# Token stages of a two-layer metaformer kernel: the second product one step later and first in the order, centring and variance as 48-channel blocks in four 64x64 tiles

## The chip, the cores and the metric

The program runs on one core of one Trainium2 chip. The metric is the device time of one execution, in microseconds. Engines are named as in the profile: PE is TensorE, PEld its weight loads, DVE is VectorE, ACT is ScalarE, POOL is GpSimd, SP is SyncE, which issues most of the DMAs here. Half a per cent of the time, some 13 us, is about what a measurement of this kernel can tell from no change.

## What is computed

The input is `x`, 4 images of 48 channels and 128 x 128 pixels. Two layers follow, each a convolution block and a feed-forward block on the pixels as tokens. Cut to what matters:

```
def _qlinear(x, W, b):
    y = q_acc(jnp.einsum('bsk,nk->bsn', q_mul(x), q_mul(W)))
    return q_acc(y + q_mul(b))
h = jax.nn.relu(_qlinear(x, W1, b1))
y = _qlinear(h, W2, b2)
...
x = x + _L0_conv_ref(_ln_c(x), ...)
t = _to_tokens(x)
t = t + _L0_ffn_ref(_ln_t(t), ...)
x = _from_tokens(t, x)
x = x + _L1_conv_ref(_ln_c(x), ...)
t = _to_tokens(x)
t = t + _L1_ffn_ref(_ln_t(t), ...)
```

`q_mul` rounds to an 8-bit float (5 exponent, 2 mantissa bits), `q_acc` to a 16-bit one. `_ln_t` and `_ln_c` are layer norms over the 48 channels of a pixel. The feed-forward block goes from 48 to 192 channels and back.

## The kernel before

The program is a row of stages with a barrier between them: `expand` (norm and the first product of layer 0), `gated_conv`, `token_mix` called as mix0, `wavelet` (the convolution block of layer 1), `attention_maps`, `fusion`, and `token_mix` called again as mix1. The change touches `token_mix` alone.

`token_mix` works on 64 items (2N with N = HW/NT = 32). An item is 512 pixels of two images: image h = 0 stands on partitions 0 to 47 and image h = 1 on partitions 64 to 111, so that most tiles are 112 x 512. For each item:

- `project` (L858, L861 in mix0; L864 in mix1) makes the last product of the convolution block in `x1_bank`; `add_residual` (L1012, L1014; L1017) adds the residual and writes `x1`, which has four buffers.
- `centre_in` (L869) subtracts the channel mean by a product with the 112 x 112 matrix `center`; ACT squares the result (`square`, L932); `variance("in")` (L887) is a product with `average`, written into `x1_bank` again; ACT makes logarithm (L939, `mix_logv`) and exponential (L942, `mix_rstd`); `quantize_norm` (L1025) makes the 8-bit `xq`.
- `hide(0)` and `hide(1)` (L900) are the two halves of the first product, `round_hidden` (L949) rounds each to 16 bits, `bias_hidden` (L1031) and `quantize_hidden` (L1039) make the 8-bit `hq`.
- `show` (L912) is the second product, in `x2_bank`; `round_shown` (L955) makes `y16`; `add_shown` makes `yb` (L1045) and then `x2` (L1050), which is stored.
- In mix0 alone a second norm follows for the next stage: `centre_out` (L875), `square("out")`, `variance("out")` (L887, into `x2_bank` again), logarithm, exponential and `normalise` (L1059, `mix_xn`).

The order of the work is written out by hand. `staged` takes for each engine a list of (stage, piece); in step k every piece with stage s works on item k - s, in the order of the list. A step of the steady loop so holds one call of each piece, each for another item. The engines are held together by semaphores. Those that matter here: `show` waits for `y16_ready` and, in mix0, for `logged["out"]` (the logarithm of the step before, which reads the bank that `show` writes); `variance("in")` of item k - 1 waits for `x1_ready` of item k, since it writes the bank that `add_residual` of item k reads; `add_residual` of item k waits for `x2_ready` of item k - 4, which read the same buffer of `x1`; `hide(1)` in mix0 waits for the rounding of `hide(0)`. SP loads item k in step k and stores `x2` and `xn` some steps later, in one queue.

Of the kernel before, what the change touches and what calls it, by code (L numbers as in the profile page):

```python
# [16 lines left out]
HID = 96  # L17
# [657 lines left out]
def token_mix(nc, t, tag, src, wT, bias, res, w1T, b1, w2T, b2, dst, norm_dst):  # L675
# [9 lines left out]
    with ExitStack() as st:  # L685
        k = Bench(nc, st, tag)
        center, average = k.sb("center", [CP, CP]), k.sb("average", [CP, CP])
# [10 lines left out]
        LEAD = 12 if wide else 4  # L698
# [26 lines left out]
        bank = [k.ps(f"bank{j}") for j in range(8 - 2 - 2 * len(norms))]  # L725
# [31 lines left out]
        with nc.Block() as block:  # L757
            @block.sync
            def _(sp):
                sp.wait_ge(prepared, 1)  # L760
                sp.dma_start(center[:, :], const(t, "center")[0:CP]).then_inc(weights_in, 16)
# [56 lines left out]
                def store_norm(at):  # L818
                    sp.wait_ge(xn_ready, at.n + 3)
                    for h in range(2):  # L820
                        rows = slice(PADH * h, PADH * h + C)
# [12 lines left out]
                staged(sp, 2 * N, SLOTS, [(0, load), (4, store_x2)] + [(7, store_norm)] * wide, LEAD)  # L834
# [8 lines left out]
            def _(pe):  # L843
# [22 lines left out]

                def centre_in(at):
                    pe.wait_ge(x1_ready, at.n + 1)
                    pe.matmul(centre_bank["in"][at.pair][0:CP, :], center[:, :], x1[at.slot][:, :],  # L869
                              start=True, stop=True).then_inc(centered["in"], 1)  # L870

                def centre_out(at):
                    pe.wait_ge(x2_ready, at.n + 1 + SLOTS)
                    pe.wait_ge(xn_ready, at.n + 1)
                    pe.matmul(centre_bank["out"][at.pair][0:CP, :], center[:, :], x2[at.pair][:, :],  # L875
                              start=True, stop=True).then_inc(centered["out"], 1)

                def variance(v):
                    def piece(at):
# [7 lines left out]
                        pe.matmul(var_bank[v][0:CP, :], average[:, :], sq[v][at.pair][:, :],  # L887
# [3 lines left out]
                def hide(m):  # L891


                    def piece(at):
                        pe.wait_ge(xq_ready, at.n + 1)
                        if m == 1 and len(bank) == 2:
                            pe.wait_ge(h16_ready, 4 * at.n + 2)
# [18 lines left out]
                pieces = [(0, project), (3, show), (2, hide(0)), (2, hide(1)), (1, variance("in")), (0, centre_in)]  # L916
                if norm_dst is not None:
                    pieces = [(0, project), (3, show), (2, hide(0)), (4, centre_out), (2, hide(1)), (1, variance("in")), (5, variance("out")), (0, centre_in)]
# [3 lines left out]
            def _(act):  # L922
# [41 lines left out]
            def _(dve):  # L964
                dve.memset(eps[:, 0:1], 1e-5)
                dve.memset(eps[:, 1:2], 1e-6)
                dve.memset(w1q[:, :, :, :], 0.0)
# [60 lines left out]
                def bias_hidden(at):  # L1028
                    for m in range(2):
                        dve.wait_ge(h16_ready, 4 * at.n + 2 * m + 2)  # L1030
# [31 lines left out]
                pieces = [(0, add_residual), (3, add_shown), (2, bias_hidden), (2, quantize_hidden), (1, quantize_norm)]  # L1062
                if norm_dst is not None:
                    pieces.append((5, normalise))
# [1267 lines left out]
```

## Time and profile before

| | |
|---|---|
| median of 3 runs | 2622.84 us (2618.95 to 2629.99) |
| profiled execution | 2624.89 us |
| its span, first to last instruction | 2623.1 us |
| busy shares | PE 87%, PEld 48%, DVE 58%, ACT 43%, POOL 17% |
| mix0 in the trace | from about 812 us to 1297 us |
| mix1 in the trace | from about 2232 us to the end |

The busy time is how long an engine has an instruction under way. It is a mean over stages that have different limits, so the two token stages are read by themselves: by the busy time in windows, and by the timeline of one step, which gives for each instruction its start, its duration and what its engine waited for.

### The profile page before, as it was taken

To read this page: it belongs to the slowest core of one execution; us is meant where nothing else is said; L and a number is where in the kernel's file an instruction comes from. 1 tells how busy PE (TensorE), PEld (TensorE's weight loads), DVE (VectorE), ACT (ScalarE), POOL (GpSimd) and SP (SyncE) were. 2 spreads that over 40 slices of the span, in tenths; PEclk is the share of its full clock that TensorE was granted. 3 is DMA by queue.
4 is the path that set the end of the run, shared out by engine and by line. 5 is a ranking of instruction groups with operands and counts; after the bars stand their busy time and mean duration, and the time that the engine had idled before them with its cause. 6 is when DMAs were issued, how large, how long until landed. Compare 5 with 4: busy or idle time off the path is not lost. (4 is left out here: it accounts for less than half of the span.)

```text
span 2623.1 us, 62156 instructions
## 1 busy us (share of the span) xinstructions
PE 2272.7 (87%) x21290; PEld 1247.5 (48%) x21290; DVE 1523.5 (58%) x2653; ACT 1123.3 (43%) x2338; POOL 450.0 (17%) x707
## 2 busy tenths in 40 slices
PE   6679778898996999999699999999976998688886
PEld 3344436667773333333266666666641232233332
DVE  3345401111113777777488888888842455577776
ACT  4346421111112888888532222222211111577776
POOL 7510015100100000000054444444410000000000
PEclk9789869999997999999899999999987999899999
DMA  6999989788874777877576666666628999333332
GB/s 154 260 254 270 253 284 303 230 263 262 285 245 91 142 142 146 152 142 145 100 155 144 142 142 142 142 143 143 144 86 162 240 267 237 87 102 106 105 102 78
DMA packets 533239, 458.55 MB, mean 175 GB/s; under 512 B 316476, under 2 KB 445444, under 8 KB 529778
## 3 DMA queue, kind: packets, MB, share of 16 engines
q1 hardware_dynamic: 462882, 425.87, 63.4%
q0 software_dynamic: 5744, 23.34, 3.7%
q10 hardware_dynamic: 64512, 7.88, 2.3%
q8 instruction: 78, 1.28, 0.2%
q14 instruction: 23, 0.19, 0.0%
HBM read 272.33 MB, written 186.40 MB: 175 GB/s over the span
## 5 line engine op out<-in xcount | busy, mean ns | idle before, releaser
L604 PE MATMUL gate_ps<-gate_data,gate_wt 64*64 64x289 f32 x6144 | 397.1, 416 | 39.2 <-issue 27.2
L604 PEld LDWEIGHTS gate_ps<-gate_data,gate_wt 64*64 64x64 f32 x6144 | 303.1, 136 | 134.3 <-issue 59.8
L662 DVE TENSOR_TENSOR gate_out<-gate_gelu,gate_ps 128x578 f32<-128x578 f32 x96 | 72.2, 756 | 399.3 <-PE gate_ps L604 343.7
L949 ACT CAST mix_h<-mix_bank 96x512 f16<-96x512 f32 x512 | 267.6, 593 | 7.1 <-PE mix_bank L900 3.2
L639 ACT ACTIVATE gate_gelu<-gate_ps 128x578 f32<-128x578 f32 x96 | 62.7, 653 | 367.8 <-PE gate_ps L604 331.2
L2036 PE MATMUL fus_bank<-fus_xt,fus_taps 76*32 76x512 f32 x1344 | 159.6, 626 | 28.4 <-DMA fus_shift<-gate_shift 23.5
L1031 DVE TENSOR_SCALAR mix_hb<-mix_h,mix_b1q 96x1024 f16<-96x1024 f16 x256 | 122.7, 479 | 93.6 <-ACT mix_h L949 93.6
L900 PE MATMUL mix_bank<-mix_xq,mix_w1q 112*96 112x512 fp8e5 x512 | 143.5, 382 | 29.1 <-ACT mix_h L949 23.0
L1039 DVE CAST mix_hq<-mix_hb 96x2048 fp8e5<-96x2048 f16 x128 | 156.5, 1223 | 19.5 <-DVE mix_hb L1031 16.9
L292 DVE COPY exp_out<-exp_y 128x384 f32<-128x384 f32 x192 | 102.1, 567 | 103.5 <-PE exp_y L255 52.1
L912 PE MATMUL mix_x_bank<-mix_hq,mix_w2q 96*112 96x512 fp8e5 x512 | 136.1, 388 | 29.9 <-DVE mix_hq L1039 27.7
L255 PE MATMUL exp_y<-exp_win,exp_xb 48*128 48x192 f32 x1024 | 114.2, 359 | 49.8 <-DVE exp_out L292 30.9
L869 PE MATMUL mix_centre_in<-mix_x,mix_center 112*112 112x512 f32 x256 | 134.6, 608 | 2.1 <-DVE mix_x L1014 1.2
L1517 PE MATMUL wav_full_bank<-wav_halves,wav_base_w 80*32 80x256 f32 x2304 | 136.3, 382 | 0.1
L887 PE MATMUL mix_x_bank<-mix_sq_in,mix_average 112*112 112x512 f32 x256 | 132.9, 601 | 2.1 <-DVE mix_x L1014 1.2
L955 ACT CAST mix_y<-mix_x_bank 112x512 f16<-112x512 f32 x128 | 74.9, 585 | 139.5 <-PE mix_x_bank L912 139.5
L255 PEld LDWEIGHTS exp_y<-exp_win,exp_xb 48*128 48x128 f32 x1024 | 88.9, 199 | 89.8 <-ACT exp_out L292 53.4
L864 PE MATMUL mix_x_bank<-mix_sc,mix_proj 112*112 112x512 f32 x128 | 73.7, 658 | 58.3 <-ACT mix_logv_in L939 37.1
L1458 PE MATMUL wav_front<-wav_strips,wav_front_w 48*32 48x256 f32 x3840 | 117.3, 383 | 0.0
L1663 POOL TENSOR_TENSOR wav_pool<-wav_scaled,wav_diag 128x256 f32<-128x256 f32 x96 | 68.6, 736 | 265.0 <-ACT wav_scaled L1572 264.7
L900 PEld LDWEIGHTS mix_bank<-mix_xq,mix_w1q 112*96 112x96 fp8e5 x512 | 58.1, 123 | 116.7 <-issue 82.3
L2036 PEld LDWEIGHTS fus_bank<-fus_xt,fus_taps 76*32 76x32 f32 x1344 | 44.8, 113 | 138.2 <-issue 135.1
(226 smaller groups left out, 4050.6 us busy)
## 6 DMA issues: line engine op xcount, KB each, us to landing
y<-exp_out SPq DMA_DIRECT2D x64, 816.0 KB, 12.2
gate_data<-y SPq DMA_DIRECT2D x24, 2176.0 KB, 17.6
g<-gate_out SPq DMA_DIRECT2D x48, 578.0 KB, 4.9
mix_sc<-g SPq DMA_DIRECT2D x31, 816.0 KB
gate_wt<-wm SPq DMA_DIRECT2D x96, 256.0 KB, 8.5
wav_strips<-xp SPq DMA_DIRECT2D x96, 204.0 KB, 3.8
wav_halves<-xp SPq DMA_DIRECT2D x48, 340.0 KB
init<-wav_init SPq DMA_DIRECT2D x48, 268.0 KB, 2.4
```

The costliest lines, as they stand in the source:

```text
L255: mm = pe.matmul(ps_y[h][q % 2][:, O2 * x:O2 * (x + 1)], xb[u][rows, 2 * q + x].rearrange("c s y x -> c (s y x)"), win[rows, :], start=Tru ...
L604: mm = pe.matmul(banks(a, v)[64 * g:64 * (g + 1), r], wt[q][64 * r:64 * (r + 1), 2 * a + g, n, :], src, start=n == 0, stop=n == 3)
L869: pe.matmul(centre_bank["in"][at.pair][0:CP, :], center[:, :], x1[at.slot][:, :], start=True, stop=True).then_inc(centered["in"], 1)
L887: pe.matmul(var_bank[v][0:CP, :], average[:, :], sq[v][at.pair][:, :], start=True, stop=True).then_inc(var[v], 1)
L900: pe.matmul(bank[(2 * m + h) % len(bank)][0:HID, :], w1q[:, h, m, :], xq[at.pair][:, :], start=True, stop=True).then_inc(hidden, 1)
L912: mm = pe.matmul(x2_bank[0:CP, :], w2q[:, h, m, :], hq[at.pair][:, m, h, :], start=(h + m == 0), stop=(h + m == 2))
L949: act.copy(h16[at.pair][:, m, h, :], bank[(2 * m + h) % len(bank)][0:HID, :]).then_inc(h16_ready, 1)
L1031: relu = dve.tensor_scalar(hb[at.pair][:, m, :, :].rearrange("p h n -> p (h n)"), h16[at.pair][:, m, :, :].rearrange("p h n -> p (h n)"), ...
L1039: dve.tensor_copy(hq[at.pair][:, :, :, :].rearrange("p m h n -> p (m h n)"), hb[at.pair][:, :, :, :].rearrange("p m h n -> p (m h n)"), sa ...
L1458: x = pe.matmul(half(u, r, 0, Q0)[STRIP * g:STRIP * (g + 1)], front_w[u][64 * r:64 * r + K0, 2 + dx, :], strips[u][64 * r:64 * r + K0, g, ...
L1517: x = pe.matmul(images(full_bank[u][STRIP * g:STRIP * (g + 1), :])[:, :, e::2], base_w[u][:, e, dx, :], halves[u][:, g, :, 1 + dx:1 + dx + ...
L2036: mm = pe.matmul(bank[u][0][STRIP * s:STRIP * (s + 1), :], taps[u][0:K2, dx, :], xt[u][:, s, :, dx:dx + W], start=dx == 0, stop=dx == TAPS ...
```

## The change

- The second product and all behind it move one stage later: `show`, `round_shown` and `add_shown` from stage 3 to 4, the second norm from 4 and 5 to 5 and 6, the stores from 4 and 7 to 5 and 8.
- `show` and `add_shown` go to the head of the lists of PE and DVE (`round_shown` was at the head of ACT's list already). In mix0 `project` goes behind `hide(0)`, and `variance("out")` and `centre_out` stand next to each other.
- `centre_in` and `centre_out` are two products of 64 x 64 tiles each, which also swap the halves (image 0 goes to partitions 64 to 111 of `centre_bank` and back), `variance` two products on the diagonal tiles. `pe.sem_inc(pe_turn, 1)` stands ahead of each. The weights of `hide` and the stores of `xn` are swapped to match.
- The four hidden banks become pairs of 1024 columns: one semaphore count and one ACT copy of 1024 columns per `hide` in place of two of 512.
- `quantize_hidden` waits for `mixed` of two items before. The written-out head of mix1's loop has 8 steps in place of 4.

```
-        LEAD = 12 if wide else 4
+        LEAD = 12 if wide else 8
...
-        bank = [k.ps(f"bank{j}") for j in range(8 - 2 - 2 * len(norms))]
+        pairs = [k.ps(f"bank{j}", (128, 2 * NT)) for j in range(3 - len(norms))]
...
-                staged(sp, 2 * N, SLOTS, [(0, load), (4, store_x2)] + [(7, store_norm)] * wide, LEAD)
+                staged(sp, 2 * N, SLOTS, [(0, load), (5, store_x2)] + [(8, store_norm)] * wide, LEAD)
...
+                def exchange(v, at, x):
+                    pe.sem_inc(pe_turn, 1)
+                    pe.matmul(centre_bank[v][at.pair][PADH:CP, :], center[0:C, 0:C], x[0:C, :], start=True, stop=True)
+                    pe.matmul(centre_bank[v][at.pair][0:PADH, :], center[PADH:CP, PADH:128], x[PADH:CP, :],
+                              start=True, stop=True).then_inc(centered[v], 1)
...
-                        pe.matmul(var_bank[v][0:CP, :], average[:, :], sq[v][at.pair][:, :],
+                        pe.sem_inc(pe_turn, 1)
+                        pe.matmul(var_bank[v][0:PADH, :], average[0:C, 0:PADH], sq[v][at.pair][0:C, :], start=True, stop=True)
+                        pe.matmul(var_bank[v][PADH:CP, :], average[PADH:CP, PADH:CP], sq[v][at.pair][PADH:CP, :],
                                   start=True, stop=True).then_inc(var[v], 1)
...
-                            pe.matmul(bank[(2 * m + h) % len(bank)][0:HID, :], w1q[:, h, m, :], xq[at.pair][:, :],
-                                      start=True, stop=True).then_inc(hidden, 1)
+                            mm = pe.matmul(pairs[m % len(pairs)][0:HID, NT * h:NT * (h + 1)], w1q[:, 1 - h, m, :],
+                                           xq[at.pair][:, :], start=True, stop=True)
+                        mm.then_inc(hidden, 1)
...
-                pieces = [(0, project), (3, show), (2, hide(0)), (2, hide(1)), (1, variance("in")), (0, centre_in)]
+                pieces = [(4, show), (0, project), (2, hide(0)), (2, hide(1)), (1, variance("in")), (0, centre_in)]
...
-                        for h in range(2):
-                            act.wait_ge(hidden, 4 * at.n + 2 * m + h + 1)
-                            act.copy(h16[at.pair][:, m, h, :], bank[(2 * m + h) % len(bank)][0:HID, :]
-                                     ).then_inc(h16_ready, 1)
+                        act.wait_ge(hidden, 2 * at.n + m + 1)
+                        act.copy(h16[at.pair][:, m, :, :].rearrange("p h n -> p (h n)"), pairs[m % len(pairs)][0:HID, :]
+                                 ).then_inc(h16_ready, 1)
...
+                    if not isinstance(at.n, int) or at.n >= 2:
+                        dve.wait_ge(mixed, at.n - 1)
...
-                pieces = [(0, add_residual), (3, add_shown), (2, bias_hidden), (2, quantize_hidden), (1, quantize_norm)]
+                pieces = [(4, add_shown), (0, add_residual), (2, bias_hidden), (2, quantize_hidden), (1, quantize_norm)]
```

The order of the instructions on PE, one step of mix0's loop. Before:

```order
L858 MATMUL mix_x_bank<-mix_sc,mix_proj 48x448 x2
L861 MATMUL mix_x_bank<-mix_sc,mix_proj 48x64 x2
L912 MATMUL mix_x_bank<-mix_hq,mix_w2q 112x512 x4
L900 MATMUL mix_bank<-mix_xq,mix_w1q 96x512 x2
L875 MATMUL mix_centre_out<-mix_x,mix_center 112x512
...
L900 MATMUL mix_bank<-mix_xq,mix_w1q 96x512 x2
L887 MATMUL mix_x_bank<-mix_sq_in,mix_average 112x512
L887 MATMUL mix_x_bank<-mix_sq_out,mix_average 112x512
L869 MATMUL mix_centre_in<-mix_x,mix_center 112x512
```

and with the change, from its `show` on (its line numbers are those of the changed kernel):

```order
L919 MATMUL mix_x_bank<-mix_hq,mix_w2q 112x512 x4
L906 MATMUL mix_bank<-mix_xq,mix_w1q 96x512 x2
L858 MATMUL mix_x_bank<-mix_sc,mix_proj 48x448 x2
L861 MATMUL mix_x_bank<-mix_sc,mix_proj 48x64 x2
L892 MATMUL mix_x_bank<-mix_sq_out,mix_average 64x512
L893 MATMUL mix_x_bank<-mix_sq_out,mix_average 48x512
L869 MATMUL mix_centre_out<-mix_x,mix_center 48x512
L870 MATMUL mix_centre_out<-mix_x,mix_center 64x512
L906 MATMUL mix_bank<-mix_xq,mix_w1q 96x512 x2
L892 MATMUL mix_x_bank<-mix_sq_in,mix_average 64x512
L893 MATMUL mix_x_bank<-mix_sq_in,mix_average 48x512
L869 MATMUL mix_centre_in<-mix_x,mix_center 48x512
```

`show` stood behind `project` and now opens the step; the second norm's variance came behind the first norm's and now stands with its centring ahead of the second half of `hide`.

The order on DVE, the head of a step of mix0's loop. Before:

```order
L1012 TENSOR_TENSOR mix_x<-mix_x_bank,mix_rs 112x4x7x16
L1014 TENSOR_TENSOR mix_x<-mix_x_bank,mix_rs 112x64
L1045 TENSOR_SCALAR mix_yb<-mix_y,mix_b2q 112x512
L1050 TENSOR_TENSOR mix_x<-mix_yb,mix_x 112x512
L1030 ISA
```

and with the change:

```order
L1054 TENSOR_SCALAR mix_yb<-mix_y,mix_b2q 112x512
L1059 TENSOR_TENSOR mix_x<-mix_yb,mix_x 112x512
L1004 REGISTER_ALU
L1019 TENSOR_TENSOR mix_x<-mix_x_bank,mix_rs 112x4x7x16
L1021 TENSOR_TENSOR mix_x<-mix_x_bank,mix_rs 112x64
```

The addition of the residual, which came first, now stands behind the two instructions of `add_shown`.

## Rows read from the trace of the kernel before

**Rows 1.** Windows: length, busy PE, PEld, DVE, ACT, POOL (instructions), PE clock, DMA, GB/s.

```profile
10.00:20.00 10.00, 6.03 (x7) 2.27 (x8) 0.00 (x0) 1.72 (x3) 9.70 (x13) 1.00 0.65 105
720.00:800.00 80.00, 77.90 (x1243) 61.43 (x1239) 15.09 (x20) 12.40 (x19) 0.00 (x0) 0.98 0.62 215
900.00:1260.00 360.00, 335.53 (x1237) 139.05 (x1235) 281.41 (x466) 316.44 (x569) 0.00 (x0) 1.00 0.77 147
2260.00:2600.00 340.00, 285.29 (x847) 115.04 (x847) 265.50 (x423) 253.25 (x482) 0.00 (x0) 1.00 0.37 103
```

**Rows 2.** Timeline of PE in mix0: start us, us, engine, line, operation [idle before].

```profile
1007.08 1.02 PE L887 MATMUL mix_x_bank<-mix_sq_in,mix_average 112*112 112x512 f32 x2
...
1008.80 1.02 PE L869 MATMUL mix_centre_in<-mix_x,mix_center 112*112 112x512 f32 x2
1009.75 0.98 PE L858 MATMUL mix_x_bank<-mix_sc,mix_proj 96*48 96x448 f32 x4
...
1010.77 1.07 PE L912 MATMUL mix_x_bank<-mix_hq,mix_w2q 96*112 96x512 fp8e5 x4
1011.68 0.60 PE L900 MATMUL mix_bank<-mix_xq,mix_w1q 112*96 112x512 fp8e5 x2
...
1014.01 1.02 PE L887 MATMUL mix_x_bank<-mix_sq_in,mix_average 112*112 112x512 f32 x2
```

**Rows 3.** Timeline of ACT in the same step of mix0.

```profile
1008.14 0.69 ACT L939 ACTIVATE mix_logv_in<-mix_x_bank,mix_eps 112x512 f32<-112x512 f32 x1
...
1009.40 0.67 ACT L939 ACTIVATE mix_logv_out<-mix_x_bank,mix_eps 112x512 f32<-112x512 f32 x1
...
1011.88 0.58 ACT L955 CAST mix_y<-mix_x_bank 112x512 f16<-112x512 f32 x1 [0.66 <-PE mix_x_bank L912]
```

**Rows 4.** Timeline of DVE in the same step of mix0.

```profile
1011.37 0.95 DVE L1012 TENSOR_TENSOR mix_x<-mix_x_bank,mix_rs 112x448 f32<-112x448 f32 x1
1012.23 0.27 DVE L1014 TENSOR_TENSOR mix_x<-mix_x_bank,mix_rs 112x64 f32<-112x64 f32 x1
1012.50 0.35 DVE L1045 TENSOR_SCALAR mix_yb<-mix_y,mix_b2q 112x512 f16<-112x512 f16 x1
1012.88 0.69 DVE L1050 TENSOR_TENSOR mix_x<-mix_yb,mix_x 112x512 f32<-112x512 f16 x1
```

**Rows 5.** Timeline of one step of mix1: PE and ACT.

```profile
2406.99 1.04 PE L912 MATMUL mix_x_bank<-mix_hq,mix_w2q 96*112 96x512 fp8e5 x4 [0.29 <-DVE mix_hq L1039]
...
2408.07 0.58 ACT L955 CAST mix_y<-mix_x_bank 112x512 f16<-112x512 f32 x1 [1.39 <-PE mix_x_bank L912]
2408.55 2.04 ACT L949 CAST mix_h<-mix_bank 96x512 f16<-96x512 f32 x4
2410.46 0.72 ACT L939 ACTIVATE mix_logv_in<-mix_x_bank,mix_eps 112x512 f32<-112x512 f32 x1
2411.21 0.63 ACT L942 ACTIVATE mix_rstd_in<-mix_logv_in 112x512 f32<-112x512 f32 x1
2411.74 0.58 ACT L932 ACTIVATE mix_sq_in<-mix_centre_in 112x512 f32<-112x512 f32 x1
```

**Rows 6.** Timeline of DVE in the same step of mix1.

```profile
2405.62 1.22 DVE L1039 CAST mix_hq<-mix_hb 96x2048 fp8e5<-96x2048 f16 x1 [0.15 <-DVE mix_hb L1031]
...
2407.37 0.74 DVE L1017 SCALAR_TENSOR_TENSOR mix_x<-mix_x_bank,mix_pbias,mix_rs 112x512 f32<-112x512 f32 x1
2408.69 0.35 DVE L1045 TENSOR_SCALAR mix_yb<-mix_y,mix_b2q 112x512 f16<-112x512 f16 x1 [0.59 <-ACT mix_y L955]
2409.19 0.69 DVE L1050 TENSOR_TENSOR mix_x<-mix_yb,mix_x 112x512 f32<-112x512 f16 x1
...
2411.26 1.22 DVE L1039 CAST mix_hq<-mix_hb 96x2048 fp8e5<-96x2048 f16 x1 [0.15 <-DVE mix_hb L1031]
```

**Rows 7.** Line L567 of gated_conv: duration ns min/median/max, first and last start us.

```profile
L567 PE MATMUL gate_ps<-gate_maps x20: 1056/1056/1057, 341.2 to 345.5; 2*32 2x512 f32 x20
```

**Rows 8.** Waits of SP's queue in steady mix0: us in total, times, longest.

```profile
SPq L816 <- DVE mix_x L1050: 127.6, 50, 5.1
```

More of the change, by code:

```diff
@@ L686, in token_mix @@
         k = Bench(nc, st, tag)
-        center, average = k.sb("center", [CP, CP]), k.sb("average", [CP, CP])
+        center, average = k.sb("center", [CP, 128]), k.sb("average", [CP, CP])
         eps = k.sb("eps", [128, 2])
@@ L820, in store_norm @@
                     for h in range(2):
-                        rows = slice(PADH * h, PADH * h + C)
+                        rows = slice(PADH * (1 - h), PADH * (1 - h) + C)
                         def keep(y, first, n):
@@ L865, in project @@
                     mm.then_inc(projected, 1)
+                def exchange(v, at, x):
[3 more added lines that the diff above has]
+                              start=True, stop=True).then_inc(centered[v], 1)
                 def centre_in(at):
                     pe.wait_ge(x1_ready, at.n + 1)
-                    pe.matmul(centre_bank["in"][at.pair][0:CP, :], center[:, :], x1[at.slot][:, :],
-                              start=True, stop=True).then_inc(centered["in"], 1)
+                    exchange("in", at, x1[at.slot])
                 def centre_out(at):
@@ L874, in centre_out @@
                     pe.wait_ge(xn_ready, at.n + 1)
-                    pe.matmul(centre_bank["out"][at.pair][0:CP, :], center[:, :], x2[at.pair][:, :],
-                              start=True, stop=True).then_inc(centered["out"], 1)
+                    exchange("out", at, x2[at.pair])
                 def variance(v):
@@ L895, in piece @@
                         pe.wait_ge(xq_ready, at.n + 1)
-                        if m == 1 and len(bank) == 2:
-                            pe.wait_ge(h16_ready, 4 * at.n + 2)
+                        if m == 1 and len(pairs) == 1:
+                            pe.wait_ge(h16_ready, 2 * at.n + 1)
                         pe.sem_inc(pe_turn, 1)
                         for h in range(2):
-                            pe.matmul(bank[(2 * m + h) % len(bank)][0:HID, :], w1q[:, h, m, :], xq[at.pair][:, :],
-                                      start=True, stop=True).then_inc(hidden, 1)
+                            mm = pe.matmul(pairs[m % len(pairs)][0:HID, NT * h:NT * (h + 1)], w1q[:, 1 - h, m, :],
+                                           xq[at.pair][:, :], start=True, stop=True)
+                        mm.then_inc(hidden, 1)
                     return piece
@@ L914, in show @@
                     mm.then_inc(mixed, 1)
-                pieces = [(0, project), (3, show), (2, hide(0)), (2, hide(1)), (1, variance("in")), (0, centre_in)]
+                pieces = [(4, show), (0, project), (2, hide(0)), (2, hide(1)), (1, variance("in")), (0, centre_in)]
                 if norm_dst is not None:
-                    pieces = [(0, project), (3, show), (2, hide(0)), (4, centre_out), (2, hide(1)), (1, variance("in")), (5, variance("out")), (0, centre_in)]
+                    pieces = [(4, show), (2, hide(0)), (0, project), (6, variance("out")), (5, centre_out), (2, hide(1)), (1, variance("in")), (0, centre_in)]
                 staged(pe, 2 * N, SLOTS, pieces, LEAD)
@@ L966, in _ @@
                 dve.memset(eps[:, 1:2], 1e-6)
+                dve.memset(center[:, CP:128], 0.0)
                 dve.memset(w1q[:, :, :, :], 0.0)
```

10 lines of the change are left out of this document (5 added, 5 removed).

## The prediction

> **What bounds the kernel now.** I read the busy time in windows first, then the timeline of one step of each token stage, engine by engine, then the waits of SP's queue. The four rows of windows are a stretch of the first stage, one of gated_conv, steady mix0 and steady mix1. In steady mix0 PE is busy 335.5 of 360 us, ACT 316.4 and DVE 281.4; in steady mix1 PE 285.3 of 340, DVE 265.5 and ACT 253.3 [rows 1]. No engine is full, so the length of a step comes from a round of waits. A step of mix0 lasts 6.93 us, from one variance product to the next (1007.08 to 1014.01) [rows 2]. A step of mix1 lasts 5.64 us (2405.62 to 2411.26) [rows 6]. What holds mix1 there can be followed in rows: `show` starts at 2406.99, y16 at 2408.07, the four hidden roundings at 2408.55 for 2.04 us, then bias and hq, which starts at 2411.26 and ends at 2412.48; 0.15 us later the next `show` can start, which is 5.64 us after the last [rows 5, 6]. So mix1 goes in a round show, y16, h16, hq, show. In mix0 PE has 335.5/360 of the step, 6.46 us.
>
> **What the change takes away.** In PE's own time a lot. A 112 x 112 f32 product of 512 columns holds PE for 0.86 us (two products between 1007.08 and 1008.80) [rows 2]. Centring and variance as four 64 x 64 tiles can share that: in gated_conv 1243 matmul records of 64 x 64 tiles fit in 77.9 us, 0.063 us each [rows 1], though each is 289 columns long. If the two pairs in mix0 and the one in mix1 do so, PE saves 2 x 0.86 = 1.72 us a step in mix0 and 0.86 in mix1. Each change between tile shapes costs something: from centre (full) to `project` (48-column tiles) 0.95 us pass in place of 0.86 [rows 2], 0.09 more; mix0 has three such changes more than before (five in place of two), mix1 two. Taken at 0.09 to 0.15 each, PE needs 6.46 - 1.72 + 0.4 = about 5.1 us of a step in mix0. In mix1 the round show, y16, h16, hq, show is cut as well, since hq has a whole step more to wait. The single copy of 1024 columns in place of two of 512 saves ACT the gap between them, under 0.1 us each; ACT isn't full, so I count nothing; nor for the written-out steps of mix1.
>
> **What the change adds: a round within one step.** This decides. With stage 4, `add_shown` works on item k - 4 in step k, and `add_residual` of item k needs exactly that x2 (four buffers of x1) and stands behind it on DVE. Before, x2 of item k - 4 came in step k - 1, so the residual never waited for it. Now all of this must happen in turn, in mix0:
> 1. `show` start to y16 start: 1010.77 to 1011.88, 1.11 us [rows 2, 3].
> 2. y16 to yb: 1011.88 to 1012.50, 0.62 [rows 3, 4].
> 3. yb to x2: 0.38 [rows 4].
> 4. x2 to the residual's addition: 0.69 for x2 itself, plus a handover. A plain handover is 0.04 (y16 ends at 1012.46, yb starts at 1012.50) [rows 3, 4]; where a semaphore instruction stands between, it is 0.15 (hq ends at 2406.84, `show` starts at 2406.99) [rows 5, 6]. The addition has several waits ahead of it; I take the middle, 0.10: 0.79.
> 5. The addition: 0.86 to its second part, which lasts 0.27: 1.13 [rows 4].
> 6. Handover to `variance("in")`, which now has a semaphore instruction ahead: 0.15, as in 4.
> 7. Variance start to logarithm start: 1007.08 to 1008.14, 1.06 [rows 2, 3]. For the first matmul after a change of tile shape I add 0.07.
> 8. Logarithm over the exponential to the second norm's logarithm: 1008.14 to 1009.40, 1.26 [rows 3].
> 9. That logarithm lasts 0.67, and `show` of the next step waits for it with 0.15: 0.82 [rows 3].
>
> Sum: 1.11 + 0.62 + 0.38 + 0.79 + 1.13 + 0.15 + 1.13 + 1.26 + 0.82 = 7.39 us, against 6.93 now. It begins and ends with `show` of successive steps, so the step can't be shorter, whatever PE saves. A second way round is close behind: `show` 0.91 (1010.77 to 1011.68), `hide(0)` with half its matmuls 0.45 and a change of shape 0.1, `project` 1.02 (1009.75 to 1010.77) [rows 2], the variance and centring of the second norm 1.13, square 0.5 and h16 0.9 (by the spacing of ACT's copies, 2.04 us for four [rows 5]), then points 8 and 9 (2.08): 7.1. PE's saving so becomes idle time at the head of `show`.
>
> In mix1 the round closes on ACT: y16 to yb 0.62 [rows 5, 6], yb to x2 0.50, x2 0.79, addition 0.74 [rows 6], 0.15, variance 1.13, logarithm to exponential 0.75, to the square 0.53, the square to y16 about 0.49 (as y16 to h16, 0.48) [rows 5]: 5.70 us, against 5.64.
>
> The round needs all stages: in mix0 from about the seventh step on, 57 steps; in mix1 some 60. 57 x (7.39 - 6.93) = 26.2; 60 x 0.06 = 3.6; one stage more at the end of each call, about 1 us each, since a lone item's chain is what lasts there: 2. In all +32 us.
>
> **SP's queue.** The stores move one stage later with x2 and xn. Now SP waits 127.6 us in mix0 at the store of x2, with the next loads behind it [rows 8]; with x2 made early in the step and its store one stage on, the loads go out sooner. It costs nothing; it may save a few short waits for `mix_sc`, which I leave out. DMA isn't the bound at a share of 0.77 in a step that gets longer [rows 1]. The new wait of `quantize_hidden` for `mixed` is for a `show` at the head of the same step, long done.
>
> **A rule against the change.** The variance pair writes both row halves into one PSUM bank. In gated_conv, L567 does that too, on four diagonal tiles: 20 products of 1.056 us each start within 4.3 us [rows 7], so they run beside each other, and I count full overlap. The Trainium skill, "TensorEngine Tiling (Array Packing)" (Gotcha 1: PSUM Pressure), says that different row tiles can't access one PSUM bank at the same time and software must keep them apart. The row speaks against it for different partitions of a bank; were it to hold as a delay, the sum would be that of the third rival.
>
> **The rivals.**
> *Shorter links, no change.* Same rounds, but DVE starts the addition before x2 ends, as neighbours on it do (0.86 after the start of a 0.95 one [rows 4]), so 0.60 in place of 0.79; no extra 0.07 at the variance; yb to x2 in mix1 0.38 as in mix0. Steps of 7.13 and 5.32: 57 x 0.20 - 60 x 0.32 + 2 = -6 us: 2617 for the median. It decides if mix1's round comes out below about 5.5. Against it: the addition waits for x2's semaphore, which is given at its end.
> *Throughput, faster.* If some link of the round isn't there (the residual not held by x2), the fullest engine sets the step: ACT 316.4/360 x 6.93 = 6.1, less 0.1 for the copies, in mix0; DVE 265.5/340 x 5.64 = 4.4 in mix1 [rows 1]. 57 x -0.93 + 60 x -1.24 + 2 = -125: 2498. It is what the change looks like by busy time alone; against it stands the order on DVE.
> *Tiles one after another, slower.* The variance's two tiles in turn add 0.86 to both rounds: 57 x 1.32 + 60 x 0.92 + 2 = +132: 2755. Against it: rows 7.
> *A lower clock, slower.* PE would be busy some 70% of a step, with gaps of about 2 us ahead of `show`. If the granted clock fell to 1.2 GHz, `show` and variance would each take 0.86 longer in mix0, the variance in mix1: +181: 2804. In both stages the clock was full throughout; a stretch with PE busy 60% had it too [rows 1].
>
> **The numbers.** The profiled execution took 2624.89 us, 2.05 over the median. 2624.9 + 32 - 2 = 2655. Bounds of the forecast: handover in point 4 at 0.04 and no 0.07 gives 7.26 and 5.57, +16, 2639; at 0.15 and with dearer changes of shape 7.5 and 5.75, +42, 2665. Chances: forecast 0.71, shorter links 0.12, throughput 0.05, tiles in turn 0.07, clock 0.05. The last three lie outside; the range goes from the short-links case to a little above the upper bound, 2616 to 2670. Slower by over 0.5% (above 2636) is the forecast but for 0.02, and two rivals: 0.81; within 0.5% 0.14; faster 0.05.
>
> **What would show it.** A step of mix0 near 7.4 us, of mix1 near 5.7, read from variance to variance. PE idle before `show` in mix0, released by the second norm's logarithm. DVE idle before yb, released by y16, then yb, x2 and the addition without a break. PE idle before the variance, released by the addition. The four tiled products of a pair starting within some 0.1 us and then 0.43 later. Wrong if the steps are shorter than 6.9 and 5.5, if the variance takes 1.9 us to its logarithm, or if the clock falls.

## The result, and the profile after

The change takes 2930.37 us (median of 5 runs), the kernel before 2622.84 (median of 5). The ratio is 1.1103, with an interval of 1.1041 to 1.1166. Of the change's five executions one took 4399.85 us, which stays unexplained and is left out of the ratio, and the profiled one lies 30 us above the median, as do those of several experiments (up to 37), so lengths read from traces are set against each other and not against medians. The forecast was 2655 us, range 2616 to 2670: the direction was right, the size was not. The loss is some 290 us by the ratio, 307 between the medians, in place of 32.

The profiled execution of the change took 2959.97 us, its span 2958.2. The page, busy shares and the slices for PE and its clock:

```profile
PE 2461.4 (83%) x22058; PEld 1224.0 (41%) x22058; DVE 1543.2 (52%) x2655; ACT 1126.8 (38%) x2082; POOL 467.1 (16%) x707
...
PE   6689598899967878877876999999994998577877
...
PEclk9789589999955555555555999999996899789898
```

A slice is 74 us. From the 12th to the 22nd slice PEclk reads 5, half of full speed: this is mix0, which now lasts from 842 to 1551 us, counted from its first to its last logarithm of the first norm, with a little on either side. The windows show both token stages (columns as in [rows 1]), mix0 first, then mix1:

```profile
900.00:1260.00 360.00, 290.89 (x996) 80.13 (x992) 175.90 (x280) 192.53 (x280) 0.00 (x0) 0.51 0.47 87
2600.00:2920.00 320.00, 254.63 (x954) 93.15 (x954) 242.93 (x373) 224.08 (x320) 0.00 (x0) 0.87 0.36 98
```

Against [rows 1] the granted clock in steady mix0 went from 1.00 (2.4 GHz) to 0.51 (1.2 GHz but for a few us), and in mix1 to 0.87. Summed over mix0, the trace has 682 of 709 us at half clock; before, 2 of 435.

The clock is already at half when mix0 begins, in both kernels: PE waits 20 us ahead of the stage for its first load, and the clock goes down in that wait (at 812 us before, at 815 with the change). Before, it was back at 839 us, 12 us after the first product. With the change it comes back at 965 for the first time, and falls again 7 us later with PE at work. The window of 840 to 860 us, before and then after:

```profile
840.00:860.00 20.00, 17.00 (x72) 7.13 (x68) 14.95 (x26) 14.33 (x27) 0.00 (x0) 1.00 0.59 109
```

```profile
840.00:860.00 20.00, 14.57 (x49) 3.97 (x50) 7.89 (x14) 8.02 (x11) 0.00 (x0) 0.50 0.50 87
```

Where the time went, by the distance from the first to the last of the 64 logarithms of a stage: mix0 435 to 709 us, 274 more; mix1 355 to 374, 19 more. The stretch between the two, nearly all of it in stages whose code was not changed, took 980 us before and 1017 here; over the profiled executions of all kernels of this case it varies from 980 to 1023, and it is 1020 in one that has no tiled product, so I don't count these 37 us to the change. Mix0 holds nearly all of the rest.

One step of mix0 at 1.2 GHz, PE's timeline:

```profile
1099.47 1.06 PE L906 MATMUL mix_bank<-mix_xq,mix_w1q 112*96 112x512 fp8e5 x2
1100.46 1.74 PE L858 MATMUL mix_x_bank<-mix_sc,mix_proj 96*48 96x448 f32 x4
...
1102.34 1.11 PE L892 MATMUL mix_x_bank<-mix_sq_out,mix_average 48*64 48x512 f32 x1
...
1104.26 1.09 PE L906 MATMUL mix_bank<-mix_xq,mix_w1q 112*96 112x512 fp8e5 x2
1105.28 1.11 PE L892 MATMUL mix_x_bank<-mix_sq_in,mix_average 48*64 48x512 f32 x1
1105.28 1.09 PE L893 MATMUL mix_x_bank<-mix_sq_in,mix_average 48*48 48x512 f32 x1
1105.29 1.09 PE L869 MATMUL mix_centre_in<-mix_x,mix_center 48*48 48x512 f32 x1
1105.30 1.11 PE L870 MATMUL mix_centre_in<-mix_x,mix_center 48*64 48x512 f32 x1
1106.17 1.06 PE L893 MATMUL mix_x_bank<-mix_sq_in,mix_average 48*48 48x512 f32 x1
...
1109.48 1.92 PE L919 MATMUL mix_x_bank<-mix_hq,mix_w2q 96*112 96x512 fp8e5 x4 [2.21 <-ACT mix_logv_out L946]
1111.19 1.06 PE L906 MATMUL mix_bank<-mix_xq,mix_w1q 112*96 112x512 fp8e5 x2
```

and ACT's of the same step:

```profile
1107.30 0.69 ACT L946 ACTIVATE mix_logv_in<-mix_x_bank,mix_eps 112x512 f32<-112x512 f32 x1 [0.91 <-PE mix_x_bank L893]
1108.02 0.63 ACT L949 ACTIVATE mix_rstd_in<-mix_logv_in 112x512 f32<-112x512 f32 x1
1108.55 0.67 ACT L946 ACTIVATE mix_logv_out<-mix_x_bank,mix_eps 112x512 f32<-112x512 f32 x1
```

The reader is to see a closed round. `show` to `hide(0)` 1.71 (1109.48 to 1111.19); `hide(0)` to `project` 0.99; to the tiled group of the second norm 1.88; to `hide(1)` 1.92; to the tiled group of the first norm 1.02; to its logarithm 2.02; to the second norm's logarithm 1.25; and 0.93 to the next `show`. The sum is 11.72 us, the step measured. All links but the last two are PE's own work at half speed (the one to the first norm's logarithm with a handover of 0.07 to ACT). PE then idles 2.21 us for the logarithms. DVE shows that the round is not the one of the forecast:

```profile
1100.72 0.69 DVE L1059 TENSOR_TENSOR mix_x<-mix_yb,mix_x 112x512 f32<-112x512 f16 x1
1102.46 0.97 DVE L1019 TENSOR_TENSOR mix_x<-mix_x_bank,mix_rs 112x448 f32<-112x448 f32 x1 [1.04 <-PE mix_x_bank L861]
```

The addition of the residual starts 1.05 us after x2 has ended, and waits for `project`, not for x2.

### The profile page after: what moved, and what is told of

Same layout as the page of the kernel before. It is cut to its first block and busy times, and to the rows that moved or that the text cites. A ratio compares the mean times of both kernels' runs of the same rounds, so it can differ in the third digit from the quotient of the medians.

```text
span 2958.2 us, 63329 instructions
## 1 busy us (share of the span) xinstructions
PE 2461.4 (83%) x22058; PEld 1224.0 (41%) x22058; DVE 1543.2 (52%) x2655; ACT 1126.8 (38%) x2082; POOL 467.1 (16%) x707
## 5 line engine op out<-in xcount | busy, mean ns | idle before, releaser
L919 PE MATMUL mix_x_bank<-mix_hq,mix_w2q 96*112 96x512 fp8e5 x512 | 200.5, 533 | 135.4 <-ACT mix_logv_out L946 134.0
L955 ACT CAST mix_h<-mix_bank 96x1024 f16<-96x1024 f32 x256 | 251.9, 1009 | 112.1 <-PE mix_bank L906 112.0
L892 PE MATMUL mix_x_bank<-mix_sq_in,mix_average 48*64 48x512 f32 x256 | 196.7, 859 | 57.2 <-DVE mix_x L1024 54.7
L906 PE MATMUL mix_bank<-mix_xq,mix_w1q 112*96 112x512 fp8e5 x512 | 212.1, 530 | 30.9 <-DVE mix_xq L1032 30.9
L919 PEld LDWEIGHTS mix_x_bank<-mix_hq,mix_w2q 96*112 96x112 fp8e5 x512 | 75.0, 171 | 336.7 <-issue 327.4
L870 PE MATMUL mix_centre_in<-mix_x,mix_center 48*64 48x512 f32 x256 | 201.4, 879 | 0.0
L869 PE MATMUL mix_centre_in<-mix_x,mix_center 48*48 48x512 f32 x256 | 196.6, 860 | 2.2 <-DVE mix_x L1021 1.3
L893 PE MATMUL mix_x_bank<-mix_sq_in,mix_average 48*48 48x512 f32 x256 | 195.9, 857 | 0.0
L906 PEld LDWEIGHTS mix_bank<-mix_xq,mix_w1q 112*96 112x96 fp8e5 x512 | 70.9, 161 | 228.3 <-issue 217.9
L946 ACT ACTIVATE mix_logv_in<-mix_x_bank,mix_eps 112x512 f32<-112x512 f32 x128 | 88.0, 687 | 103.6 <-PE mix_x_bank L893 103.2
```

Of the source, the lines that this page charges most:

```text
L869: pe.matmul(centre_bank[v][at.pair][PADH:CP, :], center[0:C, 0:C], x[0:C, :], start=True, stop=True)
L870: pe.matmul(centre_bank[v][at.pair][0:PADH, :], center[PADH:CP, PADH:128], x[PADH:CP, :], start=True, stop=True).then_inc(centered[v], 1)
L892: pe.matmul(var_bank[v][0:PADH, :], average[0:C, 0:PADH], sq[v][at.pair][0:C, :], start=True, stop=True)
L893: pe.matmul(var_bank[v][PADH:CP, :], average[PADH:CP, PADH:CP], sq[v][at.pair][PADH:CP, :], start=True, stop=True).then_inc(var[v], 1)
L906: mm = pe.matmul(pairs[m % len(pairs)][0:HID, NT * h:NT * (h + 1)], w1q[:, 1 - h, m, :], xq[at.pair][:, :], start=True, stop=True)
L919: mm = pe.matmul(x2_bank[0:CP, :], w2q[:, h, m, :], hq[at.pair][:, m, h, :], start=(h + m == 0), stop=(h + m == 2))
```

## The experiments

What had to be found out was why the clock is low, and whether the rounds of the forecast are there once it isn't. The theories as they stood at the start: idle time of PE at the head of `show` keeps the clock low (theory I), or the tiled products themselves do (theory II). All steps below are distances of successive first-norm logarithms.

### The order alone, the tiles alone

The change's order and waits with full products:

```
-                    pe.sem_inc(pe_turn, 1)
-                    pe.matmul(centre_bank[v][at.pair][PADH:CP, :], center[0:C, 0:C], x[0:C, :], start=True, stop=True)
-                    pe.matmul(centre_bank[v][at.pair][0:PADH, :], center[PADH:CP, PADH:128], x[PADH:CP, :],
+                    pe.matmul(centre_bank[v][at.pair][0:CP, :], center[:, 0:CP], x[:, :],
...
-                        pe.sem_inc(pe_turn, 1)
-                        pe.matmul(var_bank[v][0:PADH, :], average[0:C, 0:PADH], sq[v][at.pair][0:C, :], start=True, stop=True)
-                        pe.matmul(var_bank[v][PADH:CP, :], average[PADH:CP, PADH:CP], sq[v][at.pair][PADH:CP, :],
+                        pe.matmul(var_bank[v][0:CP, :], average[:, :], sq[v][at.pair][:, :],
```

> The change with centring and variance as single 112x112 products again; its order, copies and waits stay. Theory I (the clock falls because PE stands idle for a third of each step): at the full clock a step of mix0 would be 7.9 us with PE busy some 82%, about what steady mix1 had before (84%) at the full clock, so the clock is held or falls only now and then; near 2670 us. Theory II (the clock falls because 48-channel tiles use little of the array, however long PE has them under way): the clock is full in both stages, steps 7.9 and 5.45, 2623 + 57 + (-12) = 2670 us. If neither holds and the order alone takes the clock down: mix0 at 1.2 GHz, about 13 us a step, over 2950 us.

Measured: 2691.01 us, ratio 1.0218 [1.0161, 1.0275]. The window of mix0 and two PE instructions:

```profile
1000.00:1240.00 240.00, 196.06 (x721) 80.91 (x720) 166.59 (x269) 176.68 (x270) 0.00 (x0) 1.00 0.68 127
```

```profile
1107.90 1.04 PE L915 MATMUL mix_x_bank<-mix_hq,mix_w2q 96*112 96x512 fp8e5 x4 [1.45 <-DVE mix_hq L1044]
...
1112.57 1.02 PE L889 MATMUL mix_x_bank<-mix_sq_in,mix_average 112*112 112x512 f32 x2
```

PE is busy 196.06 of 240 us and idles 1.45 ahead of `show`, at a clock of 1.00. In the same window of the change it is busy 193.46 of 240, at 0.50. The same share of busy time goes with either clock (at half clock each product lasts longer, so it is not the same work in that time). Over the whole of mix0 32 of 508 us are at half clock, most of them at its start. The steps are 8.0 us in mix0 and 5.5 to 5.7 in mix1.

The reverse, the tiled products in the order, banks and waits of before:

```
-                    pe.matmul(centre_bank["in"][at.pair][0:CP, :], center[:, :], x1[at.slot][:, :],
-                              start=True, stop=True).then_inc(centered["in"], 1)
+                    exchange("in", at, x1[at.slot])
...
-                        pe.matmul(var_bank[v][0:CP, :], average[:, :], sq[v][at.pair][:, :],
+                        pe.sem_inc(pe_turn, 1)
+                        pe.matmul(var_bank[v][0:PADH, :], average[0:C, 0:PADH], sq[v][at.pair][0:C, :], start=True, stop=True)
+                        pe.matmul(var_bank[v][PADH:CP, :], average[PADH:CP, PADH:CP], sq[v][at.pair][PADH:CP, :],
```

> The kernel before with centring and variance as 64x64 tiles; order, stages, banks and copies of before. Theory I: PE would be busy some 78% of a step of 6.6 us in mix0 and 70% in mix1, with no long gap before the second product; the clock mostly holds in mix0, 2623 - 20 = about 2600 us. Theory II: the clock falls as in the change, mix0 at 11.6 us a step, mix1 partly slower: about 2900 us.

Measured: 2905.17 us, ratio 1.1001 [1.0922, 1.1079]. The window of mix0:

```profile
900.00:1260.00 360.00, 360.00 (x1037) 100.58 (x1036) 181.56 (x292) 204.49 (x356) 0.00 (x0) 0.50 0.48 91
```

PE has no idle time at all, 360.00 of 360 us (at half speed its work fills the step, so this is partly the low clock's own doing, but a lack of work it is not), and the clock stays at 0.50: 694 of 694 us of the stage, steps of 11.1. Theory I falls in both directions: idle time without tiles costs no clock, and tiles without idle time do. The tiled products alone carry most of the loss. The Trainium skill, "TensorE: Matmul & The Clock Gate" (What's actually happening), says that throttled is the default state and that activity releases the throttle. If busy time is taken for that activity, this row disagrees.

### Filling the idle time with products of four shapes

To see with what work the clock comes back, one product on constants was put into the idle stretch ahead of `show` in mix0's loop. Nothing reads its result; it is written to `x1_bank`, after the wait for the first norm's logarithm.

```
+        fill = k.sb("fill", [CP, NT])
...
+                    if norm_dst is not None and not isinstance(at.n, int):
+                        pe.wait_ge(logged["in"], at.n + 5)
+                        pe.matmul(x1_bank[0:CP, :], average[:, :], fill[:, :], start=True, stop=True)
...
+                dve.memset(fill[:, :], 0.5)
```

> The change, and in mix0's loop one more 112x112 f32 product of 512 columns on constants, into the bank of the first norm once its logarithm has read it, ahead of the second product; nothing reads its result. Theories I and II both say that the clock comes back, if the added 0.86 us are enough: steps of 7.4 us in place of 11.7, 52 x 4.3 = 220 us faster than the change although it does more, near 2700 us. If it isn't enough, the step at 1.2 GHz grows by the 1.7 us less the gap, some 0.3 us: 2945 us.

Measured: 2718.62 us, ratio 1.0308 [1.0241, 1.0376]. The kernel does more work than the change and is some 210 us faster. Its steps in mix0 grow from 8.6 to 11.7 us until the filler begins (about step 12), then they are 7.5 and 7.6 in turn at full clock. Of the 513 us of mix0 127 are at half clock, nearly all of them before 970 us; the first filler starts at 953. mix1, which has no filler, is much as in the change: the median step is 5.65 us against 5.70, with 62 us at half clock against 86.

This filler gives PE both more rows and columns of the array and less idle time. So three more were run: a 48 x 64 tile, all 112 rows with 64 columns, and 48 rows with all 112 columns. Each has 512 moving columns, like the first, and one semaphore instruction ahead, which the first lacks. (The last two have 2 timed runs each, the others 4.)

```
# 48 rows x 64 columns
pe.matmul(x1_bank[0:PADH, :], average[0:C, 0:PADH], fill[0:C, :], start=True, stop=True)
# 112 rows x 64 columns
pe.matmul(x1_bank[0:PADH, :], average[:, 0:PADH], fill[:, :], start=True, stop=True)
# 48 rows x 112 columns
pe.matmul(x1_bank[0:CP, :], average[0:C, :], fill[0:C, :], start=True, stop=True)
```

> The change with the filler of the run before made one 48x64 tile (48 rows of the array, 64 columns) of 512 columns, at the same place; a semaphore instruction stands ahead of it. Same time on PE, a fifth of the array. Theory I (idle time): as the full filler, 2719 us. Theory II (share of the array in use): the clock stays at 1.2 GHz in mix0; 2910 to 2950 us.

> The filler with all 112 rows and 64 columns of the array. Theory II in the form that only rows count: as the full filler, 2719 us. In the form that rows times columns count: in between, the clock in mix0 partly or not restored, 2750 to 2950 us.

> The filler with 48 rows and all 112 columns. Only rows count: 2930 us. Only columns count: 2719 us. Rows times columns: as with all rows and 64 columns.

| filler, rows x columns | us | ratio | step in mix0 | half clock in mix0 |
|---|---|---|---|---|
| none (the change) | 2930.37 | 1.1103 [1.1041, 1.1166] | 11.72 | 682 of 709 |
| 112 x 112 | 2718.62 | 1.0308 [1.0241, 1.0376] | 7.5, 7.6 | 127 of 513 |
| 48 x 64 | 2957.19 | 1.1328 [1.1273, 1.1383] | 12.27 | 686 of 726 |
| 112 x 64 | 2736.46 | 1.047 [1.0384, 1.0556] | 7.5, 7.6 | 127 of 513 |
| 48 x 112 | 2968.26 | 1.1357 [1.1262, 1.1452] | 12.35 | 734 of 748 |

The windows of mix0 (48 x 64, then 112 x 64, then 48 x 112), one fence for each kernel:

```profile
1000.00:1240.00 240.00, 221.92 (x689) 57.27 (x689) 114.10 (x182) 125.34 (x182) 0.00 (x0) 0.53 0.45 85
```

```profile
1000.00:1240.00 240.00, 201.82 (x1080) 65.32 (x1081) 177.00 (x287) 190.69 (x287) 0.00 (x0) 1.00 0.71 135
```

```profile
1000.00:1240.00 240.00, 223.46 (x656) 59.78 (x658) 109.75 (x176) 121.25 (x177) 0.00 (x0) 0.50 0.44 81
```

The filler of all rows brings the clock back to 1.00 with 64 columns as well as with 112. The two of 48 rows leave it at 0.53 and 0.50, although PE is then busier (222 and 223 of 240 us against 202). Part of that is the low clock's own doing, so the shares have to be compared at one clock. The kernels with fillers of 48 rows have between them four stretches at full clock in mix0, of some 13.7 us; here is one of each (48 x 64, then 48 x 112), and then a window of the 112 x 112 filler:

```profile
1114.00:1127.70 13.70, 11.21 (x63) 3.50 (x60) 10.03 (x16) 10.53 (x16) 0.00 (x0) 1.00 0.46 99
```

```profile
1401.60:1415.30 13.70, 11.33 (x64) 3.66 (x60) 10.04 (x16) 10.53 (x17) 0.00 (x0) 1.00 0.47 100
```

```profile
1114.00:1127.70 13.70, 11.41 (x61) 3.81 (x60) 10.52 (x17) 10.63 (x17) 0.00 (x0) 1.00 0.79 149
```

PE is busy 11.2 to 11.4 of 13.7 us at full clock in all three; right behind it the first two fall back to half clock, the third stays at full up to 1355 us, 5 us before mix0's last logarithm. So what sets the fillers that bring the clock back apart from those that don't is the rows that they use, not their columns and not the time that PE is busy. The runs tell that much; the rule behind it is not settled. Low products side by side are not enough by themselves to lower the clock. The tiles of gated_conv are 64 rows high, and four of them side by side ran at 0.98 [rows 1]. In `expand` of the kernel before, products of 48 rows and 128 columns run in pairs, and the clock is full:

```profile
180.00:300.00 120.00, 112.63 (x624) 59.66 (x624) 68.93 (x126) 72.94 (x126) 0.00 (x0) 1.00 0.97 261
```

There they cover 52 of the 120 us, and products of 112 x 112 another 67. The four tiles here are 48 rows high, and stand between products of other shapes, none of 112 x 112. Other heights, other shares of the step and other data were not tried.

### The round at full clock

The first filler's kernel is the nearest thing to the change at 2.4 GHz, so its timeline tells whether the forecast's round is there. PE:

```profile
1104.06 1.04 PE L923 MATMUL mix_x_bank<-mix_hq,mix_w2q 96*112 96x512 fp8e5 x4 [0.33 <-ACT mix_logv_out L950]
1104.94 0.60 PE L907 MATMUL mix_bank<-mix_xq,mix_w1q 112*96 112x512 fp8e5 x2
1105.46 0.97 PE L859 MATMUL mix_x_bank<-mix_sc,mix_proj 96*48 96x448 f32 x4
...
1106.48 0.64 PE L893 MATMUL mix_x_bank<-mix_sq_out,mix_average 48*64 48x512 f32 x1
...
1107.50 0.63 PE L907 MATMUL mix_bank<-mix_xq,mix_w1q 112*96 112x512 fp8e5 x2
1108.25 0.61 PE L893 MATMUL mix_x_bank<-mix_sq_in,mix_average 48*64 48x512 f32 x1
...
1111.53 1.04 PE L923 MATMUL mix_x_bank<-mix_hq,mix_w2q 96*112 96x512 fp8e5 x4 [0.33 <-ACT mix_logv_out L950]
```

ACT and DVE of the same kernel, by their own views:

```profile
1105.14 0.59 ACT L965 CAST mix_y<-mix_x_bank 112x512 f16<-112x512 f32 x1 [0.19 <-PE mix_x_bank L923]
...
1109.35 0.69 ACT L950 ACTIVATE mix_logv_in<-mix_x_bank,mix_eps 112x512 f32<-112x512 f32 x1 [0.18 <-PE mix_x_bank L894]
...
1110.61 0.67 ACT L950 ACTIVATE mix_logv_out<-mix_x_bank,mix_eps 112x512 f32<-112x512 f32 x1
```

```profile
1105.76 0.35 DVE L1059 TENSOR_SCALAR mix_yb<-mix_y,mix_b2q 112x512 f16<-112x512 f16 x1 [0.57 <-ACT mix_y L965]
1106.14 0.69 DVE L1064 TENSOR_TENSOR mix_x<-mix_yb,mix_x 112x512 f32<-112x512 f16 x1
1106.97 0.97 DVE L1024 TENSOR_TENSOR mix_x<-mix_x_bank,mix_rs 112x448 f32<-112x448 f32 x1
1107.84 0.27 DVE L1026 TENSOR_TENSOR mix_x<-mix_x_bank,mix_rs 112x64 f32<-112x64 f32 x1
```

yb, x2 and the addition run without a break, as foretold. Link by link, measured against forecast: `show` to y16 1.08 (1.11), to yb 0.62 (0.62), to x2 0.38 (0.38), to the addition 0.83 (0.79), the addition 1.14 (1.13), to the variance 0.14 (0.15), to the logarithm 1.10 (1.13), to the second logarithm 1.26 (1.26), to `show` 0.92 (0.82). The sum is 7.47 us against 7.39. The filler ends 0.33 us ahead of `show` and doesn't delay it.

The kernel with full products has the second way round instead, through PE's order: 0.88, 0.53 and 1.02 to the second norm's pair, 1.81 for the pair, 0.43 to the variance, 1.16 and 1.25 to the logarithms and 0.98 to `show`: 8.06 (1107.90 to 1115.96). (The row of `show` names hq as what it waited for, since that ended last. But `show` works two stages behind hq, so it reads an hq made a step earlier than that one; what it waited for is the logarithm, which ended 0.1 us before the hq named.) With tiles the pair takes 1.02 in place of 1.81 (1106.48 to 1107.50), 0.79 less, and the first round takes over. That is all that the tiles bring at full clock in mix0, about 0.5 us of a step, and it does not make up for the order.

### Versions without the longer round

With full products again, the order of before in mix0 but for `hide(0)` ahead of `show`, and wide copies:

```
-                    pieces = [(0, project), (3, show), (2, hide(0)), (4, centre_out), (2, hide(1)), (1, variance("in")), (5, variance("out")), (0, centre_in)]
+                    pieces = [(0, project), (2, hide(0)), (3, show), (4, centre_out), (2, hide(1)), (1, variance("in")), (5, variance("out")), (0, centre_in)]
...
-                    pieces = [(3, round_shown), (2, round_hidden(0)), (4, square("out")), (2, round_hidden(1)), (1, root("in")), (5, root("out")), (0, square("in"))]
+                    pieces = [(2, round_hidden(0)), (3, round_shown), (4, square("out")), (2, round_hidden(1)), (1, root("in")), (5, root("out")), (0, square("in"))]
```

> From the kernel before: full products and the stages of before; of the change only the copies of 1024 columns stay. New in mix0: the first half of the first product stands ahead of the second product on PE, and its rounding ahead of y16 on ACT, so that the second half no longer waits for that rounding. By the rows of before the 0.44 us wait of a step of mix0 goes: steps of 6.55 in place of 6.93, 60 x 0.38 = 23 us, and in mix1 0.1 us less of rounding in the round show, y16, h16, hq, show: 6 us; near 2600 against 2629. Rival: the chain show, y16, x2, centre_out becomes the bound: no gain in mix0.

Measured: 2626.18 us, ratio 1.0021 [0.9985, 1.0057], no difference. The steps of mix0 alternate between 6.5 and mostly 7.2 to 8.1; four of 9.5 to 10.1 fall where the clock dips to half (25 of 452 us). The waits name what is late:

```profile
PE mix_x_bank L858 <- DMA mix_sc<-g: 29.5, 23, 1.7
```

Every second step `project` waits for its input, up to 1.7 us: the gain of the shorter steps went into waits on SP's queue, in which the loads stand behind the store of x2 [rows 8]. So the stores were moved one stage later, as the change has them:

```
-                staged(sp, 2 * N, SLOTS, [(0, load), (4 if wide else 4, store_x2)] + [(7, store_norm)] * wide, LEAD)
+                staged(sp, 2 * N, SLOTS, [(0, load), (5 if wide else 4, store_x2)] + [(8, store_norm)] * wide, LEAD)
```

> The run with the first half of the first product ahead of the second, and SP's stores in mix0 one stage later (5 and 8 in place of 4 and 7), so that the loads aren't queued behind a store that waits for x2. In that run every second step of mix0 was some 1.1 us longer, at a wait for mix_sc. If SP's queue is the cause: all steps 6.55 us, 28 x 1.1 = 31 us less, near 2595. If the DMA engines are: no change.

Measured: 2598.01 us, ratio 0.9906 [0.9866, 0.9946]. The steps of mix0 are 6.52 to 6.58, and the wait for `mix_sc` is gone from the list.

For mix1, the change's order with the new round opened: 8 buffers of `x1` in place of 4, and the addition of the residual ahead of `add_shown`; mix0 in the order of before, with wide copies; full products.

```
-        x1 = [k.sb(f"x1{u}", [CP, NT]) for u in range(4)]
+        x1 = [k.sb(f"x1{u}", [CP, NT]) for u in range(4 if wide else 8)]
...
-        SLOTS = 4
+        SLOTS = 4 if wide else 8
...
-                staged(sp, 2 * N, SLOTS, [(0, load), (4 if wide else 4, store_x2)] + [(7, store_norm)] * wide, LEAD)
+                staged(sp, 2 * N, SLOTS, [(0, load), (4 if wide else 5, store_x2)] + [(7, store_norm)] * wide, LEAD)
...
-                pieces = [(0, project), (3, show), (2, hide(0)), (2, hide(1)), (1, variance("in")), (0, centre_in)]
+                pieces = [(4, show), (0, project), (2, hide(0)), (2, hide(1)), (1, variance("in")), (0, centre_in)]
...
-                pieces = [(0, add_residual), (3, add_shown), (2, bias_hidden), (2, quantize_hidden), (1, quantize_norm)]
+                pieces = [(0, add_residual), (4, add_shown), (2, bias_hidden), (2, quantize_hidden), (1, quantize_norm)]
```

> Full products in both stages. mix0 in its order of before, with the copies of 1024 columns. mix1 in the change's order, but x1 has eight buffers and the residual's addition stands ahead of yb and x2 on DVE again, so that the round y16, yb, x2, addition, variance, logarithm, exponential, square, y16 is open. If that round set mix1's step in the run with full products (5.55 us), the step falls to 5.2: 60 x 0.35 = 21 us, and near 2600 against 2624. Rival (the step was set by PE, or by ACT): no change, 5.5 us a step, near 2617.

Measured: 2593.24 us, ratio 0.989 [0.985, 0.993]. mix1 goes in steps of 5.22 us; with the round in place (the change's order, full products) they were 5.51 to 5.69, and 5.64 before. mix0 is 6.87. DVE in mix1, one step:

```profile
2402.26 1.22 DVE L1044 CAST mix_hq<-mix_hb 96x2048 fp8e5<-96x2048 f16 x1 [0.18 <-DVE mix_hb L1034]
2407.48 1.22 DVE L1044 CAST mix_hq<-mix_hb 96x2048 fp8e5<-96x2048 f16 x1 [0.18 <-DVE mix_hb L1034]
```

hq follows hq by 5.22. This shows the round in mix1: with the stages of the change kept and what closes it taken away, the 64 items take 21.5 us less (350.1 to 328.6), 0.34 a step. Last, both together, mix0 with its stores moved and mix1 with its round opened:

> Both together: mix0 at 6.55, mix1 at 5.2 us a step. 2624 - 60 x 0.38 - 60 x 0.42 = 2576.

Measured: 2570.65 us, ratio 0.9847 [0.9753, 0.994], steps of 6.52 and 5.22. It is faster than the kernel before, and so than the change. The window of mix0:

```profile
1000.00:1240.00 240.00, 232.24 (x877) 101.34 (x874) 200.07 (x330) 216.19 (x331) 0.00 (x0) 1.00 0.79 149
```

PE is now busy 232 of 240 us (before, 335.5 of 360), so in mix0 little is left to gain by order alone.

## Why the prediction was wrong, and where it was right

**The step that failed** is the sentence on the clock: "In both stages the clock was full throughout; a stretch with PE busy 60% had it too." I took PE's busy share as what holds the clock, so the sum had nothing for it, and I gave the case 0.05. In its place mix0 ran at 1.2 GHz for 682 of 709 us, in steps of 11.72 us and not 7.39.

The stretch that I leaned on, 10 to 20 us, I also misread. Its window prints a clock of 1.00, but this trace's record of the clock begins at 20.1 us, so nothing stands behind that figure. The products say otherwise:

```profile
13.97 3.76 PE L236 MATMUL exp_c<-exp_xt,exp_center 112*112 112x512 f32 x4 [9.75 <-DMA exp_win<-in_winT_dram]
...
25.81 1.97 PE L236 MATMUL exp_c<-exp_xt,exp_center 112*112 112x512 f32 x4 [0.21 <-DVE exp_xb L369]
```

The same four products take 3.76 us inside the stretch and 1.97 behind it, so the stretch ran at about half clock. Even read rightly it says nothing on tiles, and the case was not one of idle time at all: the clock stayed low with PE busy all of the time, and full with full products at the same share of busy time as in the change. What the trace of before has of 48-row products side by side, the pairs in `expand`, stands among as many products of 112 x 112 and at full clock. The change takes the last products of 112 x 112 out of mix0; no row bore on that, and I should have priced it higher.

**The direction** was right, but in the change itself it is the clock's doing: of the forecast's round nothing binds there in mix0. At full clock it would have come out too (7.5 to 7.6 us a step against 6.93).

**The price of that rival** was wrong as well: 2804 us against 2930. I kept the round of the forecast and lengthened two of its links by 0.86, 9.11 us a step. At 1.2 GHz the bound is the second way round, named in the forecast at 7.1, in which nearly every link is PE's own and doubles: 11.72. So in mix0 the rival's term was 57 x (9.11 - 6.93) = 124 us, measured 274. In mix1 it was 60 x 0.92 = 55, measured 19, since the clock fell there for part of the time only.

**The round within one step** was right, in both stages. In mix0 it measured 7.47 against 7.39, no link off by more than 0.1, but it shows only where the clock is held up, not in the change's own mix0. In mix1 it is in the change wherever the clock is full: steps of 5.55 to 5.76 against 5.70, the addition 0.80 after x2 (0.79 forecast). DVE and PE of one such step:

```profile
2701.77 0.69 DVE L1059 TENSOR_TENSOR mix_x<-mix_yb,mix_x 112x512 f32<-112x512 f16 x1 [0.17 <-DVE mix_yb L1054]
2702.57 0.75 DVE L1024 SCALAR_TENSOR_TENSOR mix_x<-mix_x_bank,mix_pbias,mix_rs 112x512 f32<-112x512 f32 x1
```

```profile
2703.56 0.61 PE L892 MATMUL mix_x_bank<-mix_sq_in,mix_average 48*64 48x512 f32 x1 [1.28 <-DVE mix_x L1024]
2703.57 0.63 PE L893 MATMUL mix_x_bank<-mix_sq_in,mix_average 48*48 48x512 f32 x1
```

Where the clock is down in mix1 (86 of 374 us), steps are 5.9 to 7.0; that is where the 19 us come from.

**PE's own saving** was right and worth little: the pair takes 0.79 less at full clock, where 0.86 less a dearer change of shape was put in. The low clock then took all of it back: at 1.2 GHz the same pair lasts 1.92, more than the 1.81 of the full products at 2.4.

**The other rivals.** Tiles one after another, given 0.07, fell: the two tiles of the variance, in one bank, start 0.01 us apart in the rows above, and the logarithm follows 1.10 after the variance, not 1.9. On the Trainium skill's rule in "TensorEngine Tiling (Array Packing)" (Gotcha 1: PSUM Pressure), that row tiles can't use one bank at the same time, no run here shows a delay for tiles on different partitions. Shorter links and throughput fell with the measured 0.83 and 0.80 between x2 and addition. SP's queue, which I counted at nothing, is nothing in the change, where steps are long; at steps of 6.5 it costs about 1% (ratio 1.0021 against 0.9906).

## What to carry to other kernels

After a product is split into tiles to save TensorE time, look at the granted clock of the stage first: here 48-row tiles in place of 112-row products kept it at half for a whole stage, with TensorE busy 81% of the time or 100%. Where the record of the clock has no entry, go by how long a known product lasts. Price a lower clock on every round through the engine, not only on the one that binds at full clock. And when a stage number moves, look for the buffer that closes a round within one step; more buffers and an exchange of two pieces opened it here.

## What the runs showed of the hardware

- The granted clock stayed at 1.2 GHz with TensorE busy 360.00 of 360 us and much of the work in tiles of 48 rows, and was at 2.4 GHz with it busy 196.06 of 240 in products of 96 and 112 rows. It was at 2.4 GHz too where pairs of 48 rows stood among products of 112 x 112 (52 and 67 of 120 us).
- One product of 112 rows a step, with 64 or 112 columns, was enough to bring it back (steps of 11.7 us to 7.5); one of 48 rows, with as many columns, was not, at the same busy share at full clock (11.2 to 11.4 of 13.7 us). So work that nothing reads made this kernel some 210 us faster.
- Four tiles of 48 rows on two banks can start within 0.02 us of each other, and have their second pass 0.44 to 0.48 us later at 2.4 GHz and 0.88 to 0.91 at 1.2.
- A semaphore instruction ahead of a product that waits costs about 0.1 us: without it the filler started 0.05 us after the end of the logarithm that it waits for, with it (112 x 64) 0.14 to 0.15.
